# Token scatter into fixed expert regions, chunk by chunk during routing

## The reference

```python
logits = layernorm(x) @ router_w.T            # 2080 x 32
rw, sel = top_k(softmax(logits), 4)           # weights and experts of each token
rw = rw / sum(rw)
for e in range(32):
    h = silu(x @ gate_w[e].T) * (x @ up_w[e].T)
    acc += weight_of(e)[:, None] * (h @ down_w[e].T)
```

## Time and profile before

| | us |
|---|---|
| median of 3 runs | 3008.19 (3007.95 to 3009.06) |
| the profiled execution | 3007.99 |
| its span, first to last instruction | 3006.4 |
| mean granted clock of PE | 0.897 |
| PE / DVE / ACT / POOL busy | 2464.7 / 1930.0 / 1407.9 / 1205.3 |
| routing block | 1654 to 1788 |
| scatter, to the first load of expert rows | 1789 to 1899 |
| expert tiles | 1899 to 2370 |

### The profile page before, as it was taken

The page is one execution under the profiler, slowest core; times in us unless marked ns, Lnnn a source line. Parts: engine busy times, 40 slices in busy tenths (PEclk is TensorE's granted clock), DMA queues, the critical chain, the costliest instruction groups (busy, mean ns, idle before and its releaser), DMA issues. The chain is left out here.

```text
span 3006.4 us, 48030 instructions
## 1 busy us (share of the span) xinstructions
PE 2464.7 (82%) x17070; PEld 2086.0 (69%) x17071; DVE 1930.0 (64%) x2723; ACT 1407.9 (47%) x3465; POOL 1205.3 (40%) x757
## 2 busy tenths in 40 slices
PE   4999996788888888888887730699999689999986
PEld 4999996788878888888876520344444367777775
DVE  7566434999999999999998360122222257677653
ACT  0342327878888888888875210011111123333432
POOL 3100003666666666666665017200000345554331
PEclk9988978999999999999999855799999778899996
DMA  5700000000000110000000016456555321111000
GB/s 204 318 1 1 1 1 29 30 30 31 30 31 30 38 45 37 30 31 30 30 30 1 7 62 199 133 173 223 197 174 172 99 54 29 47 42 31 8 8 15
DMA packets 63511, 201.49 MB, mean 67 GB/s; under 512 B 12346, under 2 KB 17594, under 8 KB 60474
## 3 DMA queue, kind: packets, MB, share of 16 engines
q1 hardware_dynamic: 25210, 96.31, 9.3%
q0 software_dynamic: 26272, 80.77, 8.4%
q10 hardware_dynamic: 11808, 21.50, 1.9%
HBM read 130.31 MB, written 68.23 MB: 66 GB/s over the span
## 5 line engine op out<-in xcount | busy, mean ns | idle before, releaser
L841 POOL TENSOR_TENSOR m_hs<-m_hs,m_BC 128x1040 f32<-128x1040 f32 x256 | 619.0, 2418 | 381.8 <-DVE m_hs L954 381.8
L760 ACT ACTIVATE m_dA<-m_dt,m_A 128x128 f32<-128x128 f32 x2048 | 614.3, 393 | 185.1 <-DVE m_hs L954 110.5
L635 PE MATMUL m_py<-m_hs,ident 128*128 128x130 f32 x4096 | 530.1, 284 | 146.7 <-POOL m_hs L841 146.7
L954 DVE TENSOR_TENSOR_SCAN m_hs<-m_dA,m_own 128x1040 f32<-128x1040 f32 x256 | 593.2, 2317 | 35.5 <-ACT m_dA L760 22.3
L635 PEld LDWEIGHTS m_py<-m_hs,ident 128*128 128x128 f32 x4096 | 496.9, 197 | 166.2 <-POOL m_hs L841 164.0
L939 DVE TENSOR_TENSOR m_own<-m_BC,m_own 128x1040 f32<-128x1040 f32 x256 | 318.7, 1245 | 17.9 <-DVE m_own L911 3.2
L587 PE MATMUL m_pw<-m_xg,m_w_in 128*128 128x130 f32 x2048 | 273.7, 294 | 51.3 <-DVE m_xc L902 34.9
L587 PEld LDWEIGHTS m_pw<-m_xg,m_w_in 128*128 128x128 f32 x2048 | 264.9, 210 | 55.0 <-DVE m_xc L902 37.9
L1384 PE MATMUL e_pG<-e_w_gu,e_xT 128*128 x656 | 235.2, 502 | 10.9 <-issue 7.0
L1364 POOL DMA_DIRECT2D e_x<-slots x80 | 42.9, 536 | 403.1 <-PE e_pX L1375 396.3
L1384 PEld LDWEIGHTS e_pG<-e_w_gu,e_xT 128*128 128x128 f32 x656 | 119.7, 192 | 91.5 <-issue 25.3
(11 more groups left out here) (272 smaller groups left out, 4609.6 us busy)
## 6 DMA issues: line engine op xcount, KB each, us to landing
m_BC<-xs SPq DMA_DIRECT2D x16, 2080.0 KB, 10.0
slots<-a_zero POOLq DMA_DIRECT2D x48, 512.0 KB, 38.9
e_w_gu<-in_gate_up_w SPq DMA_DIRECT2D x32, 768.0 KB, 5.2
e_x<-slots POOLq DMA_DIRECT2D x82, 256.0 KB, 2.9
slots<-e_y ACTq DMA_DIRECT2D x82, 256.0 KB, 2.6
e_w_d<-in_down_w SPq DMA_DIRECT2D x32, 256.0 KB, 5.7
out_h<-t_ho SPq DMA_DIRECT2D x8, 520.0 KB, 3.3
a_AT<-in_A_cols SPq DMA_DIRECT2D x8, 512.0 KB, 7.0
```

The lines of the kernel that those rows point to most:

```text
L635: mm = pe.matmul(py[k % 2][:, 0:MT], ident[:, :], hs[u % NB][:, n, :], start=False, stop=(half == 1 and n == HN - 1))
L760: act.activation(images(dA[u % NB][:, n, :])[:, :, 1:TOK], images(dt[b][:, k, :])[:, :, 1:TOK], ACT.Exp, scale=A[:, at:at + 1]).then_inc(d ...
L841: pool.tensor_tensor(hs[u % NB][:, :, :], hs[u % NB][:, :, :], BC[b][:, ST + half * HN:ST + (half + 1) * HN, :], ALU.mult).then_inc(prod_r ...
L954: dve.tensor_tensor_scan(hs[u % NB][:, :, :].rearrange("p n t -> p (n t)"), dA[u % NB][:, :, :].rearrange("p n t -> p (n t)"), bu, 0.0, AL ...
```

## The change

Each expert gets a region of its own in a new DRAM buffer `regions`, with CAP = T + 128 rows, so that a token's row is its expert's region start plus a running count, known as soon as its chunk is chosen. The chunks are written out without hardware loops. After the logits of a chunk DVE chooses (`choose`), PE forms the ranks inside the chunk on top of the running counts (`ranks`, 14 matmuls of 32 columns), DVE picks each token's row (`place`), and POOL issues the chunk's 16 indirect DMAs; of the five chunks the first EARLY = 4 are issued in the routing block and the last at the start of the expert block. An expert's rows begin 128 rows into its region; its tiles are aligned to the end of its rows, so only the first 128 rows of each region are cleared (16 more DMAs in the first stage; the 48 stay). The tail of routing works out each tile's start row (`tile_row`), which POOL reads into a register for each load, and the dense rows `slot` that the results still use. The root and reciprocal become Ln and Exp with a factor of -0.5. The constant `first` (320 KB) is replaced by `region` (16 KB), and PE waits for the constants only ahead of the first logits.

```diff
@@ -113,11 +113,16 @@
         @block.gpsimd
         def _(pool):
-            n = slots_d.shape[0] // (2 * P)
+            n = E // 2
+            regions = regions_d.rearrange("(e r) d -> e r d", r=CAP)
+            rows = slots_d.shape[0] // (2 * P)
             pool.wait_ge(setup, 11)
             pool.wait_ge(c_in, 16)
             with pool.Fori(0, n) as i:
+                pool.dma_start(regions[bass.ds(i * 2, 2), 0:P, :].rearrange("j p d -> p j d"), zero[:, :, :]).then_inc(cleared, 16)
+            with pool.Fori(0, rows) as i:
                 pool.dma_start(slots_d[bass.ds(i * 2 * P, 2 * P), :].rearrange("(j p) d -> p j d", p=P), zero[:, :, :]).then_inc(cleared, 16)
+            n += rows
...
-HALF = E * NT // 2
-def route(nc, hT, ident, mean_w, router_d, tri_d, iota_e_d, iota_j_d, first_d, x_tok, weight, slot, tile_end, tile_slot, tile_need, pairs):
+CAP = T + P
+EARLY = 4
+def scatter_chunk(pool, c, regions_d, slot_x, x_tok, scattered, slot_ready=None, tr_ready=None):
+    per = CT // TT
+    if slot_ready is not None:
+        pool.wait_ge(slot_ready, c + 1)
+        pool.wait_ge(tr_ready, (c + 1) * per)
+    for n in range(c * per, (c + 1) * per):
+        for k in range(TOPK):
+            pool.indirect_dma_start(regions_d, bass.IndirectOffsetOnAxis(ap=slot_x[:, n, k:k + 1], axis=0),
+                                    x_tok[:, n, :], None).then_inc(scattered, 16)
...
+        @block.gpsimd
+        def _(pool):
+            for c in range(EARLY):
+                scatter_chunk(pool, c, regions_d, slot_x, x_tok, scattered, slot_ready, tr_ready)
...
-            pe.wait_ge(loaded, 16 * 5)
...
+            def ranks(c):
+                pe.wait_ge(chosen_ready, c + 1)
+                pe.wait_ge(before_ready, c + 1)
+                here = chosen[c % 2]
+                for q in range(Q):
+                    to = br[0:TT, q * E:(q + 1) * E]
+                    pe.matmul(to, tri[:, :], here[:, q, :], start=True, stop=False)
+                    for m in range(q):
+                        pe.matmul(to, ones[0:TT, 0:TT], here[:, m, :], start=False, stop=False)
+                    mm = pe.matmul(to, ones[0:TT, 0:TT], before[c % 2][:, :], start=False, stop=True)
+                mm.then_inc(rank_done, 1)
...
+                if c == 0:
+                    pe.wait_ge(loaded, 16 * 5)
...
+                ranks(c)
+            pe.wait_ge(before_ready, NC + 1)
+            pe.matmul(bm[:, 0:E], ones[0:TT, :], before[NC % 2][:, :], start=True, stop=True).then_inc(count_done, 1)
...
-                act.activation(rstd[:, :], bv[:, 0:CT], ACT.Sqrt, bias=eps[:, 0:1]).then_inc(sd_ready, 1)
...
+                act.activation(rstd[:, :], bv[:, 0:CT], ACT.Ln, bias=eps[:, 0:1]).then_inc(ln_ready, 1)
+                act.wait_ge(ln_ready, c + 1)
+                act.activation(rstd[:, :], rstd[:, :], ACT.Exp, scale=-0.5).then_inc(rstd_ready, 1)
...
-                dve.reciprocal(rstd[:, :], rstd[:, :]).then_inc(rstd_ready, 1)
...
+            def choose(c):
+                here, chosen_of = slice(c * Q, (c + 1) * Q), slice(c * Q * TOPK, (c + 1) * Q * TOPK)
+                logits = lg[c % 2]
+                dve.wait_ge(lg_done, c + 1)
+                dve.tensor_copy(logits[:, :, :], bl[0:TT, 0:Q * E].rearrange("p (q e) -> p q e", q=Q)).then_inc(lg_ready, 1)
+                dve.wait_ge(lg_ready, c + 1)
+                for q in range(Q):
+                    dve.max(best[:, c * Q + q, :], logits[:, q, :]).then_inc(top_ready, 1)
+                dve.wait_ge(top_ready, (2 * c + 1) * Q)
+                for q in range(Q):
+                    dve.max_index(which[:, c * Q + q, :], best[:, c * Q + q, :], logits[:, q, :]).then_inc(top_ready, 1)
+                dve.wait_ge(top_ready, (2 * c + 2) * Q)
+                dve.tensor_copy(whichf[:, :, :], which[:, here, 0:TOPK]).then_inc(which_ready, 1)
+                dve.wait_ge(which_ready, c + 1)
+                dve.tensor_tensor(hot[:, chosen_of, :], iota_e[:, :].unsqueeze(1).broadcast_to([TT, Q * TOPK, E]),
+                                  whichf[:, :, :].rearrange("p q k -> p (q k)").unsqueeze(2).broadcast_to([TT, Q * TOPK, E]),
+                                  ALU.is_equal).then_inc(hot_ready, 1)
+                dve.wait_ge(hot_ready, c + 1)
+                dve.tensor_reduce(chosen[c % 2][:, :, :], hot[:, chosen_of, :].rearrange("p (q k) e -> p q e k", k=TOPK), AX.X, ALU.add).then_inc(chosen_ready, 1)
+                dve.wait_ge(chosen_ready, c + 1)
+                dve.tensor_reduce(csum[:, :], chosen[c % 2][:, :, :].rearrange("p q e -> p e q"), AX.X, ALU.add).then_inc(csum_ready, 1)
+                dve.wait_ge(csum_ready, c + 1)
+                dve.tensor_tensor(before[(c + 1) % 2][:, :], before[c % 2][:, :], csum[:, :], ALU.add).then_inc(before_ready, 1)
+            def place(c):
+                of = slice(c * Q * TOPK, (c + 1) * Q * TOPK)
+                dve.wait_ge(rank_done, c + 1)
+                dve.tensor_tensor(picked[:, of, :].rearrange("p (q k) e -> p q k e", k=TOPK), hot[:, of, :].rearrange("p (q k) e -> p q k e", k=TOPK),
+                                  br[0:TT, 0:Q * E].rearrange("p (q e) -> p q e", q=Q).unsqueeze(2).broadcast_to([TT, Q, TOPK, E]),
+                                  ALU.mult).then_inc(pos_ready, 1)
+                dve.wait_ge(pos_ready, c + 1)
+                dve.tensor_reduce(slotf[:, of], picked[:, of, :], AX.X, ALU.add).then_inc(slotf_ready, 1)
+                dve.wait_ge(slotf_ready, c + 1)
+                dve.tensor_copy(slot_x[:, c * Q:(c + 1) * Q, :], slotf[:, of].rearrange("p (q k) -> p q k", k=TOPK)).then_inc(slot_ready, 1)
...
+                if c + 1 < NC:
+                    deviations(c + 1)
+                choose(c)
+                place(c)
...
+            dve.tensor_copy(last[:, :], bm[:, 0:E]).then_inc(step, 1)
+            dve.wait_ge(step, 1)
+            dve.tensor_tensor(tiles[:, :], last[:, :], region[:, :], ALU.subtract).then_inc(step, 1)
...
+            dve.scalar_tensor_tensor(out=off[:, :], in0=ends[:, :], scalar=-float(P), in1=last[:, :], op0=ALU.mult, op1=ALU.add).then_inc(step, 1)
+            dve.tensor_tensor(cmp[:, :, :], ends[0:1, :].unsqueeze(1).broadcast_to([1, SLOTS, E]),
+                              iota_j[0:1, :].unsqueeze(2).broadcast_to([1, SLOTS, E]), ALU.is_le).then_inc(step, 1)
+            dve.wait_ge(step, 9)
+            dve.tensor_tensor(doff[:, 0:E - 1], off[0:1, 1:E], off[0:1, 0:E - 1], ALU.subtract).then_inc(step, 1)
+            dve.tensor_reduce(te[:, :], cmp[:, :, :], AX.X, ALU.add).then_inc(step, 1)
+            dve.wait_ge(step, 11)
+            dve.tensor_tensor(part_of[:, :, 0:E - 1], cmp[:, :, 0:E - 1], doff[:, 0:E - 1].unsqueeze(1).broadcast_to([1, SLOTS, E - 1]),
+                              ALU.mult).then_inc(step, 1)
...
+            dve.tensor_reduce(rowf[:, :], part_of[:, :, 0:E - 1], AX.X, ALU.add).then_inc(step, 1)
...
+            dve.scalar_tensor_tensor(out=tile_row[:, :], in0=rowf[:, :], scalar=off[0:1, 0:1], in1=live[:, :], op0=ALU.add, op1=ALU.mult).then_inc(step, 1)
...
+            dve.tensor_tensor(picked[:, :, :], hot[:, :, :], off[0:TT, :].unsqueeze(1).broadcast_to([TT, NT * TOPK, E]), ALU.mult).then_inc(step, 1)
+            dve.wait_ge(step, 24)
+            dve.tensor_reduce(shift[:, :], picked[:, :, :], AX.X, ALU.add).then_inc(step, 1)
+            dve.wait_ge(step, 25)
+            dve.tensor_tensor(slot[:, :, :], slotf[:, :].rearrange("p (n k) -> p n k", k=TOPK), shift[:, :].rearrange("p (n k) -> p n k", k=TOPK),
...
+        def row_of(eng, j):
+            return eng.value_load(tile_row[0:1, bass.ds(j, 1)], min_val=0, max_val=E * CAP - P)
...
-            for n in range(NT):
-                for k in range(TOPK):
-                    pool.indirect_dma_start(slots_d, bass.IndirectOffsetOnAxis(ap=slot[:, n, k:k + 1], axis=0),
-                                            x_tok[:, n, :], None).then_inc(scattered, 16)
+            for c in range(EARLY, NC):
+                scatter_chunk(pool, c, regions_d, slot_x, x_tok, scattered)
+            rows = [row_of(pool, r) for r in range(2)]
+            more = later_pairs(pool)
             pool.wait_ge(scattered, 16 * NT * TOPK)
             for r in range(2):
-                pool.dma_start(x[r][:, :], slots_d[r * P:(r + 1) * P, :]).then_inc(x_in[r], 16)
-            with pool.Fori(0, later_pairs(pool)) as i:
+                pool.dma_start(x[r][:, :], regions_d[bass.ds(rows[r], P), :]).then_inc(x_in[r], 16)
+            with pool.Fori(0, more) as i:
                 for r in range(2):
+                    row = row_of(pool, i * 2 + r + 2)
                     pool.wait_ge(x_turned, i * 2 + r + 1)
-                    pool.dma_start(x[r][:, :], slots_d[bass.ds((i * 2 + r + 2) * P, P), :]).then_inc(x_in[r], 16)
+                    pool.dma_start(x[r][:, :], regions_d[bass.ds(row, P), :]).then_inc(x_in[r], 16)
```

(59 more changed lines are left out.)

212 lines of the change are left out of this document (87 added, 125 removed).

## The result

The changed kernel takes 2951.64 us by the median of four runs (2948.0 to 2960.97), the kernel before 3008.62 (3007.95 to 3010.99) beside it: ratio 0.9814 (0.9803 to 0.9825). The forecast was 2929.7 with 2912 to 2950.

A forecast was written before the change was run, and what follows sets the result against it. The scatter, one queue of 80 indirect DMAs on POOL, bounds its stage; beside routing, routing's chain sets the block's end. First expert load at 1820.7 instead of 1898.97 saves 78.3 us: 3007.99 - 78.3 = 2929.7 us, range 2912 to 2950.

The forecast's parts named there:

- the cadence: Routing, time from chunk to chunk: 18.3 us at the high clock, 20.0 with 1.7 added, 24.0 all low.
- the landing: Between the last scatter issue and the first load of expert rows: a wait of 2.56 us.
- the first slots: Routing, first chunk's places ready for POOL to scatter: at 1688.3 us.
- routing is much slower than counted: Rival for the routing stage: unrolled code fetched late, waits between engines; 2950 to 3000 us, chance 0.06.
- Start of routing: Routing's first mean no longer waits for constants: starts at about 1654.7 us, 4.6 us earlier.
- POOL beside it: Scatter issues beside routing: 1.29 us each, 22.2 to 24 us per chunk, four chunks done at 1777 to 1784.
- a paced POOL: Rival: every issue beside routing takes 2.32 us, 64 end at 1836.8, time 2974 us; chance 0.09.
- The tail: End of routing on DVE after the fifth placing: 24.0 us, ending the block at 1792.3.
- the 16 issues: Chunk four's scatters behind the barrier on POOL: 24.7 us, including 4.3 for DVE's linear-weight preparation.
- Nothing else moved: First stage and expert loop: extra clears and register reads hidden, same number of tiles, PE's clock unaffected; zero cost.

The follow-up runs named there:

- experiment 1: Changed kernel with none of the chunks scattered in the routing block (3012.06 us, ratio 1.0011) or with all five (2941.88 us, ratio 0.9777).
- group 7: Runs together on one chip: the unedited changed kernel 2933.68 us (ratio 0.9755), and the fastest version, all five chunks in the block plus two edits, 2920.68 us (0.9708).
- experiment 2: Four kernels: plain DMAs 2922.99 us, a quarter of the scatter's bytes 2948.89, ring loads after all scatters 2950.56, scatters behind the block with POOL arithmetic inside 3019.32.
- the plain DMAs: Changed kernel with all 80 indirect scatters replaced by plain DMAs of the same bytes to fixed places, experts reading rows from 0: 2922.99 us.
- two edits of a few lines on DVE and SP: On `EARLY = 5`: w_f's load moved into the routing block, w_f's preparation split so first rows are copied earlier; 2919.51 us (0.972), later 2919.96 and 2920.68.
- group 6: Runs together on one chip: `EARLY = 5` alone 2929.49 us, with w_f's load moved into the routing block 2926.11, with w_f's preparation split too 2919.96.
- quarter: Changed kernel with 128 of each scattered row's 512 floats, same number of indirect DMAs, experts reading rows from 0: 2948.89 us.
- rings late: Changed kernel with expert weight loads for ring places 1 to 3 waiting until all 80 scatters have landed: 2950.56 us, ratio 0.9814.
- w_f moved: Changed kernel (EARLY = 4) with only the 1 MB load of w_f issued at the start of the routing block: 2950.68 us, ratio 0.982.
- split: Changed kernel with EARLY = 5 and w_f's preparation split, its load not moved: 2935.81 us, ratio 0.9764.
- group 2: Runs together on one chip: changed kernel with EARLY = 0, 3012.06 us (ratio 1.0011), and with EARLY = 5, 2941.88 us (0.9777).
- the arithmetic: EARLY = 0 kernel with 16 POOL multiplications of a private tile behind each of the first four chunks' places, no scatter in the block: 3019.32 us.

## Why the prediction came out as it did

**The step that failed is the cadence**: the prediction added up a chunk's chain as it is alone, with 0.3 us for all handovers, and let POOL beside it cost only longer issues that were hidden. The 20.0 us were the chain without scatters (20.4 measured in experiment 1). Beside them PE's signals may come late, and then a cycle takes 25.0 to 26.9. The changed kernel, unedited, measures both: 2951.64 with late signals, 2933.68 without, 18.0 us apart, by its own profiles 2948.0 and 2930.76. Of these 17.2 us the four cycles are 14.6 (99.9 against 85.3) and the landing 1.0. The forecast of 2929.7 describes the second kind, 1.1 us from its profile, but in part by luck: the first slots came 4.5 us early there, the four cycles took 5.3 more than forecast, the landing 3.6 more, and the stages behind the first load ran 2.6 us shorter than in the kernel before. The upper end of the range, 2950, allowed 24.0 us a chunk, PE all at its low level; the measured 25.0 lies outside it, and the rival "routing is much slower than counted", which holds 2951.64, had 0.06. One of its two reasons, waits between engines, is what happened, but nothing in the working priced it.

*The clock* is part of it. By the tables of stages the granted clock of the four cycles is 0.78, 0.61, 0.60, 0.63 with late signals; without scatters, over the same four cycles:

```profile
1684.00:1705.00 21.00, 19.05 (x95) 14.34 (x94) 9.94 (x26) 7.70 (x9) 0.00 (x0) 0.74 0.00 1
1705.00:1725.00 20.00, 18.07 (x95) 13.82 (x94) 9.21 (x23) 7.70 (x9) 0.00 (x0) 0.77 0.00 1
1725.00:1744.00 19.00, 15.41 (x92) 12.19 (x91) 9.21 (x23) 7.37 (x9) 0.00 (x0) 0.84 0.00 1
1744.00:1767.00 23.00, 16.42 (x85) 13.16 (x83) 7.99 (x26) 5.08 (x8) 0.00 (x0) 0.65 0.00 0
```

PE stands still longer (22.5 us of the four cycles for 14.0) and works at the lower level more of the time. How much of the 4.6 us a chunk is signals and how much is clock was not separated. By its profile in group 7 the changed kernel with signals in time has 0.74, 0.65, 0.75 and 0.75.

*Start of routing*: first slots at 1682.98, 5.3 earlier than forecast. The block itself began 1.8 earlier than before's in this execution, the first mean ran at the high clock (3.03 us, I had taken the low one from the earlier trace rows) and the logits took 3.73 for 4.85. Ln, table load and Exp took 0.61 + 1.28 + 0.55 = 2.44, forecast 2.5, in every chunk.

*POOL beside it* held: issues of 0.98 to 0.99 with 0.30 between them, single ones held to 2.65 beside DVE's operations on two tensors in SBUF, 64 issues through by about 1779.5 for 1777 to 1784. The rival of a paced POOL is out: the idle of 27.53 ahead of its last part is its slack. The Trainium skill (SBUF — State Buffer, "Who interferes with whom") has the second of the two engines wait in full; the single issues that met such an operation did, so the trace agrees, but they were too few to matter. The same section infers that an operation on two tensors leaves the making of descriptors alone; here an issue that starts beside L1234 takes 2.14 for 0.98, and the measurement decides.

*The tail* took 23.1 us for 24.0, the 16 issues 25.3 for 24.7.

*The landing* was mis-sized: 7.17 for 2.56. I took the row of a scatter with nothing beside its end; here the ring loads of the expert weights, which in the kernel before were through long ago, run beside the last issues, and experiment 2 shows that without them it is 3.02, with them and a quarter of the bytes 2.85. In the other two profiles of the changed kernel it was 5.69 and 6.13.

*Nothing else moved*, as said: the clears are hidden, and the expert stage and the last one cost what they did (from the first load to the end 1107.1 us for 1107.4). In the loop of the experts the register reads found their room: PE is busy 53.97 of the 55 us from 1860 to 1915, at a granted clock of 1.00.

## What to carry to other kernels

When a queue of work is moved beside a chain that runs over several engines, price both: the moved work beside the chain, and the chain's handovers beside the moved work. A control that leaves the work where it was but keeps the new chain (`EARLY = 0`) costs one run and splits the two at once. A cause that seems to belong to an edit must be seen twice, with the old program beside it: one group without late signals looked like the merit of a moved load, and it took two more to show that the old program had the same luck. A control must also keep the timing of what it replaces: the plain DMAs were done so early that they could not tell what they were meant to tell. And once the long wait is gone, read what the next instruction stood behind: the fifth chunk in the block and two edits of a few lines on DVE and SP brought another 13 us (2933.68 to 2920.68 in group 7), at a ratio of 0.9708; of these the two edits are 9.5 (2929.49 to 2919.96 in group 6).

## What was unexpected in the hardware

**Signals of PE that come up to 11.7 us late beside indirect DMAs.** In the runs where it happens, waits of DVE and ACT on PE end late, while a signal of DVE to POOL in the same microseconds takes 0.30 us. In most of these profiles PE's matmuls go on at their usual pace meanwhile; in three PE is held too, up to one transpose in 1.4 us. In the four profiles with the steadiest pattern (quarter, rings late, w_f moved, split) all 16 late placings begin 1.7 to 2.3 us after POOL's last issue of the previous chunk ends. That gives a cycle of its own: 1.9 us from the placing to the first issue, 21.5 for 16 issues, 2.2 until the signal comes, 25.6 us, whatever the chain needs. It takes the scatter beside routing (`EARLY = 0` beside `EARLY = 5` in group 2: none), and a quarter of its bytes is enough. Whether it takes the indirect form is open, as the rows of the plain DMAs and of the arithmetic ended before PE's ranks. It also takes something that changes from group to group and that no profile here shows: three groups had none, four had it in every program with indirect DMAs in the block. What that is stays open, and so does the way by which it holds PE; whether breaks in POOL's row of issues would help was not tried.

**The opening of a block behind DMAs in flight.** With all five chunks in the routing block, POOL's last issue ends at 1812.4 and the first load of the next block starts at 1821.87:

```profile
1811.38 0.98 POOL L1026 DMA_INDIRECT regions<-x_tok,slot_x  x1 [0.30 <-issue]
1821.87 1.20 POOL L1410 DMA_DIRECT2D e_x<-regions  x2 [9.50 <-issue]
```

9.50 us, and 9.49 or 9.50 in the six other profiles of programs with all five chunks in the block that I read, where a barrier behind an idle POOL took 1.00 (DVE's last end 1805.98 to the issue at 1806.98). Part of it is the landing.
